# Shared feed-forward moved out of a pipelined loop, its last batch split into half banks and token tiles, and loop and experts joined in one program

## The chip, the cores and the metric

The kernel runs on one core of one Trainium2 chip. The metric is the device time of one execution in microseconds. A core has five engines with queues of their own: TensorE (PE, matmuls; PEld is its weight loads), VectorE (DVE), ScalarE (ACT), GpSimd (POOL) and SyncE (SP, which only issues transfers here). They meet through semaphores. ScalarE, GpSimd and SyncE issue DMAs, which 16 DMA engines carry out.

## The reference

Input x is 8 batches of 256 tokens of 512 features, the context has the same shape. Four layers follow each other, each added to x with a gate tanh(g):

```python
x = x + tanh(g_xattn[0]) * retention(layernorm(x), ctx)       # 4 heads
x = x + tanh(g_ffn[0]) * ffn_and_expert(layernorm(x))         # relu ffn + one expert matrix
x = x + tanh(g_xattn[1]) * attention(layernorm(x), ctx, ctx)  # over features, 8 heads
x = x + tanh(g_ffn[1]) * moe(layernorm(x))                    # below
```

The last layer has a shared part and 64 routed experts of capacity 256, of which each token uses six:

```python
su = x_flat @ w_shared_up; y_s, g_s = split(su, 2)
shared = silu(g_s) * y_s @ w_shared_down
scores = sigmoid(x_flat @ w_gate); topk_idx = top_k(scores, 6)
w = scores[topk_idx] / sum
pos = running number of the token in its expert; valid = pos < 256
out_r = silu(g_r) * v_r @ w_down      # per expert, on its gathered tokens
moe = shared + sum_k w_k * out_r[expert_k, pos_k]
```

The matrices of the shared part are 512 x 256 and 128 x 512; an expert's are 512 x 128 and 64 x 512. All matmuls but those of row maxima and of positions are in float32.

## The kernel before, in words

`build` opens three blocks one after the other; at the end of each block all engines meet. `setup_and_scores` makes the first attention's matrix and stores normalized x and values to HBM. `main_loop` carries the batches through three streams of units: **F** (first attention and first feed-forward: out, turn, gate, x1, turn2, logits, up, expert, down, with layer norms stats/norm, stats2/norm2, stats3/norm3), **T** (second attention) and **R** (routing and the shared feed-forward). The order of the units is one hand-written list, `ORDER` (L409). "T.V4+2" in it means that in step s the unit T.V4 runs for batch s - 2. F has lag 0, T lags 1 and 2, R lags 2 and 3, so that steps 3 to 7 hold all units and steps 8 to 10 the rest. Each engine runs its part of each unit in this order (`steps`, L462) and waits for the others only through semaphores; there is no other planner.

PSUM has eight banks. `quad` is four of them: a unit T.S0 to T.S7 fills it with scores (L1138), VectorE takes maxima of all four at once (`maxima`, L888), T.P and T.M turn those to rows; T.Q0 to T.Q7 fill it with shifted scores (L1160, L1163), ScalarE takes the exponential of all four (`exps`, L721), T.V multiplies by the values (L1178) into `t_pV`. GpSimd sums the exponentials over four such units per group (`sum_up`, L624: four additions in each of sum0a to sum0c, sum1a to sum1c), T.Z adds over partitions (L1187), T.A0 and T.A1 (`attended`, L903) scale, and T.add0 and T.add1 on GpSimd add to x (L632). `quad` has one occupant at a time (`QUAD`, L459). Three `work` banks go round among the other units (`WORK`, L458); a unit waits until the third before it is released.

R takes the norm of a batch (r_stats, rsqrt on GpSimd L610, r_norm), turns it (L1196), makes gates (r_gates), and VectorE finds the six experts, the position of each token in them and two kinds of addresses: r_sigmoid, r_hot, r_pos (matmuls L1214, L1215), r_slots, r_places. GpSimd then scatters: R.x0 to R.x3 send the 12 rows of token tiles and places to `xs_d` by three each (L644), R.send0 to R.send3 send 12 token numbers to `ids_d` (L658). R.up (L1206, eight matmuls of 256 columns, each run in two passes), R.shared (VectorE, L932 to L938), R.down0 and R.down1 (L1221, L943) are the shared feed-forward; the store to `acc_d` on SP's queue follows (L589), and behind batch 6's the first expert weights (L578). The last batch's token numbers are sent in the third block (L1329).

`experts` takes 32 pairs of experts: SP loads 4 x 128 rows of `xs_d` into one of four buffers (L1290) and the weights (L123, L124), TensorE transposes (e_pT, L1435), multiplies up (e_pU, L1447) and down (e_pD, L1458), ScalarE and VectorE evacuate, GpSimd scatters the results by token number to `y_d` (L1340), which needs `ids_d` back in SBUF (L1311, SP's queue between the rows of pair 3 and pair 4). The **final sum** goes over 16 token tiles: SP loads six rows per token in two parts (L1306) into eight buffers, VectorE runs six scalar_tensor_tensor in a chain (L1415), ScalarE stores (L1374).

## Time and profile before

| | us |
|---|---|
| median of 3 runs | 1253.87 (1252.85 to 1258.54) |
| the profiled execution, its own time | 1244.85 |
| its span | 1243.1 |
| TensorE busy (matmuls) | 1003.2 (81%) |
| VectorE busy | 707.4 (57%) |
| GpSimd busy | 611.1 (49%) |
| ScalarE busy | 300.8 (24%) |
| mean granted clock of TensorE | 0.91 of 2.4 GHz |
| moved by DMA | 252 MB, mean 203 GB/s |

Steps of the loop begin with the matmuls of F.out0. In the profile a busy time is the time with an instruction of that kind under way; matmul ends are modelled. The clock is what was granted: 1.00 is 2.4 GHz, 0.50 is 1.2 GHz. Where a row says "[x <-engine tile]", the engine was idle for x before it, until that released it; "issue" is idle time with no wait shown.

### The profile page before, as it was taken

To read this page: it belongs to the slowest core of one execution; us is meant where nothing else is said; L and a number is where in the kernel's file an instruction comes from. 1 tells how busy PE (TensorE), PEld (TensorE's weight loads), DVE (VectorE), ACT (ScalarE), POOL (GpSimd) and SP (SyncE) were. 2 spreads that over 40 slices of the span, in tenths; PEclk is the share of its full clock that TensorE was granted. 3 is DMA by queue.
4 is the path that set the end of the run, shared out by engine and by line. 5 is a ranking of instruction groups with operands and counts; after the bars stand their busy time and mean duration, and the time that the engine had idled before them with its cause. 6 is when DMAs were issued, how large, how long until landed. Compare 5 with 4: busy or idle time off the path is not lost. (4 is left out here: it accounts for less than half of the span.)

```text
span 1243.1 us, 16070 instructions
## 1 busy us (share of the span) xinstructions
PE 1003.2 (81%) x5966; PEld 562.1 (45%) x5966; DVE 707.4 (57%) x1241; ACT 300.8 (24%) x390; POOL 611.1 (49%) x588
## 2 busy tenths in 40 slices
...
PEclk9978999999999999999999986765999999999655
DMA  4892049487380652712403015035789899994796
GB/s 183 304 356 85 1 163 385 180 294 282 136 305 12 233 196 102 273 67 102 136 2 127 27 51 187 0 131 200 251 304 330 291 344 296 328 297 172 281 419 283
DMA packets 103834, 252.24 MB, mean 203 GB/s; under 512 B 14016, under 2 KB 14400, under 8 KB 102993
## 3 DMA queue, kind: packets, MB, share of 16 engines
...
## 5 line engine op out<-in xcount | busy, mean ns | idle before, releaser
L1340 POOL DMA_INDIRECT y_d<-e_eo,e_ids x128 | 124.8, 975 | 158.5 <-DVE e_eo L1395 126.8
L624 POOL TENSOR_TENSOR t_psum<-t_psum,t_probs 128x512 f32<-128x512 f32 x128 | 162.8, 1302 | 50.8 <-ACT t_probs L721 47.8
L888 DVE TENSOR_REDUCE t_nmx<-quad 128x4 f32<-128x2048 f32 x64 | 146.5, 2289 | 62.6 <-PE quad L1138 62.4
L721 ACT ACTIVATE t_probs<-quad 128x2048 f32<-128x2048 f32 x64 | 120.2, 1877 | 174.6 <-PE quad L1163 174.4
L644 POOL DMA_INDIRECT xs_d<-r_norm,r_xaddr x96 | 95.5, 995 | 28.0 <-issue 27.7
L658 POOL DMA_INDIRECT ids_d<-r_tokk,r_addr x84 | 82.7, 984 | 42.5 <-DVEq L1003 20.9
L1160 PE MATMUL quad<-b_qry,b_key 32*128 32x512 f32 x512 | 78.8, 687 | 19.9 <-ACT t_probs L721 13.6
L1389 DVE TENSOR_TENSOR e_hT<-e_pU,e_gate 128x256 f32<-128x256 f32 x32 | 13.6, 425 | 140.5 <-ACT e_gate L1356 98.2
L1435 PE MATMUL e_pT<-ident,e_xg 128*128 128x128 f32 x512 | 72.4, 286 | 22.9 <-DMA e_xg<-xs_d 22.4
L624 POOL TENSOR_TENSOR t_psum<-t_probs 128x512 f32<-128x512 f32 x64 | 82.3, 1320 | 11.7 <-ACT t_probs L721 9.7
L1138 PE MATMUL quad<-b_key,b_qry 32*128 32x512 f32 x512 | 74.7, 654 | 16.4 <-DVE t_nmx L888 13.2
L605 POOL TENSOR_TENSOR f_rstd<-f_veps,mhalf 128x2 f32<-128x2 f32 x24 | 17.0, 707 | 144.3 <-DVE f_veps L789 144.3
L1435 PEld LDWEIGHTS e_pT<-ident,e_xg 128*128 128x128 f32 x512 | 56.7, 144 | 61.0 <-issue 26.8
L1178 PE MATMUL t_pV<-t_probs,b_cT 128*32 128x512 f32 x512 | 68.2, 620 | 0.0
L1384 DVE COPY e_xT<-e_pT 128x512 f32<-128x512 f32 x64 | 44.1, 689 | 41.0 <-PE e_pT L1435 39.6
L1057 PE MATMUL work<-f_normT,wupT 128*128 128x256 f32 x256 | 61.3, 395 | 0.0
L1057 PE MATMUL work<-b_xnT,wg 128*128 128x256 f32 x256 | 59.7, 387 | 1.6 <-DVE f_zT L808 1.6
L1395 DVE COPY e_eo<-e_pD 128x512 f32<-128x512 f32 x64 | 44.3, 692 | 28.5 <-PE e_pD L1458 25.8
L1049 PE MATMUL work<-wo,f_zT 128*128 128x512 f32 x128 | 58.6, 601 | 1.3 <-issue 1.3
L1049 PE MATMUL work<-wexp,f_normT 128*128 128x512 f32 x128 | 58.7, 601 | 0.5 <-issue 0.5
L1049 PE MATMUL work<-wdnT,f_hT 128*128 128x512 f32 x128 | 58.8, 604 | 0.0
L1057 PEld LDWEIGHTS work<-f_normT,wupT 128*128 128x128 f32 x256 | 48.9, 196 | 17.0 <-issue 10.6
...
## 6 DMA issues: line engine op xcount, KB each, us to landing
...
```

Source lines behind the costliest of these rows:

```text
L624: ins = g_.tensor_tensor(psum0[:, q, :], first[:, q, :], probs[s % NP][:, q, :], ALU.add)
L644: g_.indirect_dma_start(out=xs_d, out_offset=bass.IndirectOffsetOnAxis(ap=xaddr[b % 2][:, t, k:k + 1], axis=0), in_=normR[b % 2][:, t, :], ...
L658: g_.indirect_dma_start(out=ids_d, out_offset=bass.IndirectOffsetOnAxis(ap=addr[b % 2][:, t, k:k + 1], axis=0), in_=tokk[b % 2][:, t, k:k ...
L721: A(probs[s % NP][:, :, :], quad[:, :, :], ACT.Exp, scale=SCALE1).then_inc(W["exp_ok"], 1)
L888: V.tensor_reduce(nmx[g][:, m, :], quad[:, :, :], axis=AX.X, op=ALU.max, negate=True).then_inc(W["mx_ok"], 1)
L1049: ins = mm(dst, lhs[:, k, t * P:(t + 1) * P], w[:, k, :], start=(k == 0), stop=(k == KC - 1))
L1057: ins = mm(dst[:, j * S:(j + 1) * S], w[:, k, o * P:(o + 1) * P], rhs[:, k, :], start=(k == 0), stop=(k == KC - 1))
L1138: ins = mm(quad[:, q, :], qry[b % 2][r, g, m * P:(m + 1) * P], key[b % 2][r, g, :], start=True, stop=True)
L1160: mm(quad[:, q, :], key[b % 2][r, g, n * P:(n + 1) * P], qry[b % 2][r, g, :], start=True, stop=False)
L1178: ins = mm(pV[q * HD:(q + 1) * HD, :], cT[:, n, r:r + HD], probs[s % NP][:, q, :], start=(n == 0), stop=(n == KC - 1))
L1340: g_.indirect_dma_start(out=y_d, out_offset=bass.IndirectOffsetOnAxis(ap=ids[:, HC * p + n:HC * p + n + 1], axis=0), in_=eo[u][:, n, :], i ...
L1435: last = tr(pT[t][:, k * P:(k + 1) * P], xg[u][:, HT * e + t, k * P:(k + 1) * P], ident[:, :])
```

## The change

R.up, R.shared and R.down leave the loop. Batch b's transposed norm is stored to HBM (R.keep, SP's queue) and the store to `acc_d` now comes right behind T.add1 (R.acc), without the shared part. The list `ORDER` has a new order for steps 0 to 5; steps 6 and 7 and all that follows is one list `ENDING`, with batch numbers. In it batch 7's second attention has units L: each S and Q is split into two half units of two `quad` banks each, with occupants kept per half (`quad_holders`); the sums over exponentials are four matmuls in each L.V (into a `work` bank), so GpSimd has no sum units for this batch; and norm, turn, gates, sigmoid, hot, pos, slots, places and row scatters go by token tile (0 and 1). r_places releases the row scatters (`route_ok`) before the token numbers are made (`ids_ok`). L.up0 to L.up7 are the shared feed-forward's first matmuls for all batches, into `quad`; ScalarE's Silu and one VectorE operation make `shT`. The three `with nc.Block()` become two: loop and experts are one program per engine, without a meeting of all engines in between; each first use of a buffer there waits for its own semaphores. The experts use `quad` and `work` as their PSUM banks, and one SBUF arena for the buffers of both. In the final sum TensorE makes the shared part's second matmul and, with diagonal matrices of the weights made by ScalarE, the first three rows; VectorE chains the other three and adds TensorE's result. The diff, cut:

```diff
+            loop, kept = main_loop(nc, io, outer, mid, {**constants, **weights, **drams})
+            final = experts(nc, io, out, outer, mid, {**constants, **weights, **drams, **kept})
+            with nc.Block() as block:
+                @block.sync
+                def _(sp):
+                    loop["sync"](sp)
+                    final["sync"](sp)
...
 ORDER = [(u.split("+")[0], int(u.split("+")[1])) for u in """
+F.out0+0 T.S0+1 F.out1+0 T.V4+2 R.acc+2 F.stats+0 T.S1+1 R.keep+2 F.norm+0 T.V5+2 T.V6+2 T.V7+2 T.sum1c+2 T.S2+1 F.turnA+0 F.turnB+0
+T.add1+2 T.A1+2 T.Z1+2 T.S3+1 T.P0+1 F.gateA+0 T.S4+1 F.next+0 F.gateB+0 T.S5+1 R.send0+3 T.M0+1 R.stats+2 F.x1a+0 R.norm+2 T.S6+1 F.x1b+0
+R.turnA+2 R.send1+3 R.turnB+2 T.Q0+1 R.gates+2 F.stats2+0 R.x1+3 R.send2+3 R.x2+3 T.Q1+1 F.keys+0 T.V0+1 F.turn2A+0 R.x3+3 F.turn2B+0
+T.sum0a+1 F.norm2+0 R.send3+3 T.V1+1 T.S7+1 F.logits+0 T.sum0b+1 F.best+0 F.upA+0 F.upB+0 T.P1+1 R.sigmoid+2 R.hot+2 F.weight+0 T.M1+1
+T.Q2+1 F.expert0+0 R.slots+2 T.Q3+1 T.cT+0 F.expert1+0 R.pos+2 R.places+2 T.Q4+1 T.sum0c+1 F.down0+0 T.Q5+1 R.x0+2 F.down1+0 F.stats3+0
+T.Q6+1 F.norm3+0 T.sum1a+1 T.sum1b+1 T.V2+1 T.Z0+1 T.V3+1 T.add0+1 T.Q7+1 T.A0+1
+""".split()]
+STEPS = 6
+ENDING = [(u.split("/")[0], int(u.split("/")[1])) for u in """
...
+T.Q5/6 R.places/5 F.down1/7 T.V2/6 T.Q6/6 T.Z0/6 T.V3/6 T.Q7/6 F.stats3/7 F.norm3/7 T.V4/6 T.sum1a/6 T.V5/6 T.A0/6 L.S0a/7 L.S0b/7 T.V6/6
+T.sum1b/6 L.S1a/7 L.S1b/7 T.sum1c/6 L.S2a/7 L.S2b/7 R.x3/4 T.add0/6 L.S3a/7 L.S3b/7 T.Z1/6 L.P0/7 L.S4a/7 R.acc/5 R.acc/6 L.S4b/7 R.send0/5
+R.x0/5 T.V7/6 L.M0/7 L.S5a/7 L.S5b/7 L.Q0a/7 T.A1/6 L.Q0b/7 L.S6a/7 T.add1/6 L.S6b/7 R.stats/6 R.send1/5 L.Q1a/7 R.norm/6 L.Q1b/7 L.S7a/7
+R.x1/5 R.x2/5 L.S7b/7 R.send2/5 R.turnA/6 R.send3/5 R.turnB/6 L.Q2a/7 L.Q2b/7 R.gates/6 L.add0/7 L.M1/7 L.Q3a/7 L.P1/7 L.V0/7 R.sigmoid/6
+L.V1/7 R.x3/5 R.hot/6 L.A0/7 L.Q3b/7 R.slots/6 L.stats0/7 R.places/6 L.V2/7 L.Q4a/7 R.x0/6 L.V3/7 L.Q4b/7 L.norm0/7 R.x1/6 L.Q5a/7 L.A1/7
+R.pos/6 L.Q5b/7 L.add1/7 L.sigmoid0/7 L.stats1/7 L.hot0/7 L.V4/7 L.norm1/7 R.x2/6 L.Q6a/7 L.slots0/7 L.Q6b/7 R.keep/5 L.V5/7 R.x3/6 L.Q7a/7
+L.Q7b/7 L.places0/7 R.keep/6 L.V6/7 L.rows0/7 L.rows1/7 L.V7/7 R.send0/6 L.turn0/7 R.send1/6 R.send2/6 L.sigmoid1/7 L.gates0/7 L.pos0/7
+L.turn1/7 R.send3/6 L.gates1/7 L.up0/7 L.up1/7 L.hot1/7 L.pos1/7 L.up2/7 L.up3/7 L.up4/7 L.up5/7 L.up6/7 L.up7/7 L.slots1/7 L.places1/7
 """.split()]
...
+        def r_keep(b):
+            sp.wait_ge(W["x4T_ok"], 2 * b + 2)
+            sp.dma_start(nrT_d[b, :, :].rearrange("p (k s) -> p k s", k=KC), normRT[:, :, :]).then_inc(W["nr_kept"], 16)
...
+                A(probs[n % NP][:, 2 * h:2 * h + 2, :], quad[:, 2 * h:2 * h + 2, :], ACT.Exp, scale=SCALE1).then_inc(W["exp_ok"], 1)
...
+        act.preload_act_table(ACT.Silu)
+        for b in range(NB):
+            act.wait_ge(W["su_mm"], b + 1)
+            A(shT[:, b, :], quad[:, b % G, S:2 * S], ACT.Silu).then_inc(W["es_ok"], 1)
...
+                V.tensor_reduce(nmx[g][:, m, 2 * h:2 * h + 2], quad[:, 2 * h:2 * h + 2, :], axis=AX.X, op=ALU.max, negate=True).then_inc(W["mx_ok"], 1)
...
+                for q in range(G):
+                    r = (g * G + q) * HD
+                    mm(pV[q * HD:(q + 1) * HD, :], cT[:, n, r:r + HD], probs[s % NP][:, q, :], start=(n == 0), stop=(n == KC - 1))
+                for q in range(G):
+                    ins = mm(z[q * HD:(q + 1) * HD, :], ones32[:, :], probs[s % NP][:, q, :], start=(n == 0), stop=(n == KC - 1))
...
+        for u in range(2):
+            sp.wait_ge(W[f"xscat{u}"], 16 * T * TOPK * (NB // 2))
+        sp.wait_ge(W["pv_mm"], 8 * NB)
+        for p in range(XB):
+            load_rows(p)
+        for u in range(2):
+            sp.wait_ge(W[f"scat{u}"], 16 * T * TOPK * (NB // 2 - u))
+        sp.wait_ge(ids_sent, 16 * T * TOPK)
...
+            for k in range(HALF):
+                done = A(diag[i % 2][:, k, :], ident[:, :], ACT.Copy, scale=comb_all[:, i, k:k + 1])
+            done.then_inc(diag_ok, 1)
...
+            V.tensor_tensor(acc[:, i, :], acc[:, i, :], pD[i % HC][:, :], ALU.add).then_inc(part_ok, 1)
...
+            mm(pD[i % HC][:, :], shT[:, i // T, (i % T) * P:(i % T + 1) * P], wsd[:, :], start=True, stop=False)
+            pe.wait_ge(part_in[u], 16 * uses(j, XB + OB))
+            pe.wait_ge(diag_ok, i + 1)
+            for k in range(HALF):
+                last = mm(pD[i % HC][:, :], diag[i % 2][:, k, :], parts[u][:, k, :], start=False, stop=(k == HALF - 1))
+            last.then_inc(half_mm, 1)
```

## Rows read from the trace of the kernel before

**Rows 1.** The page's forty slices of the span: granted clock and DMA share, in tenths.
```profile
PEclk9978999999999999999999986765999999999655
DMA  4892049487380652712403015035789899994796
```

**Rows 2.** Busy us by stretch: PE, PEld, DVE, ACT, POOL; then clock, DMA share, GB/s.
```profile
384.70:467.70 83.00, 81.48 (x477) 42.43 (x473) 63.71 (x116) 23.39 (x26) 59.95 (x55) 1.00 0.46 165
...
632.80:714.50 81.70, 80.66 (x472) 42.44 (x472) 63.08 (x115) 22.67 (x26) 59.13 (x54) 1.00 0.18 59
714.50:860.50 146.00, 83.70 (x424) 35.79 (x416) 78.74 (x146) 25.36 (x26) 108.83 (x99) 0.68 0.27 101
860.50:1161.20 300.70, 254.69 (x1792) 147.77 (x1792) 100.01 (x160) 86.47 (x161) 136.51 (x140) 0.97 0.83 284
1161.20:1243.10 81.90, 0.00 (x0) 0.00 (x0) 70.83 (x96) 0.00 (x0) 0.00 (x0) 0.50 0.89 359
```

**Rows 3.** Timeline of PE in steps 4 and 5: start us, us, instructions.
```profile
393.00 3.72 PE L1057 MATMUL work<-r_normT,wsu 128*128 128x256 f32 x16
396.65 1.14 PE L1138 MATMUL quad<-b_key,b_qry 32*128 32x512 f32 x8
...
410.70 3.70 PE L1049 MATMUL work<-wo,f_zT 128*128 128x512 f32 x8
414.34 1.14 PE L1138 MATMUL quad<-b_key,b_qry 32*128 32x512 f32 x8
...
419.13 1.02 PE L1221 MATMUL work<-wsd,r_shT 128*128 128x512 f32 x2
...
463.54 1.06 PE L1178 MATMUL t_pV<-t_probs,b_cT 128*32 128x512 f32 x8
```

**Rows 4.** Timeline of POOL around the end of step 4.
```profile
466.30 0.72 POOL L605 TENSOR_TENSOR f_rstd<-f_veps,mhalf 128x2 f32<-128x2 f32 x1 [0.64 <-DVE f_veps L789]
467.07 5.33 POOL L624 TENSOR_TENSOR t_psum<-t_probs 128x512 f32<-128x512 f32 x4
...
475.39 10.09 POOL L624 TENSOR_TENSOR t_psum<-t_psum,t_probs 128x512 f32<-128x512 f32 x8
485.44 1.27 POOL L632 TENSOR_TENSOR r_acc<-f_xs,t_att 128x512 f32<-128x512 f32 x1
```

**Rows 5.** Timeline of POOL: last row scatter, first and last of batch 7's token numbers.
```profile
850.13 0.98 POOL L644 DMA_INDIRECT xs_d<-r_norm,r_xaddr  x1 [0.30 <-issue]
861.20 0.97 POOL L1329 DMA_INDIRECT ids_d<-r_tokk,r_addr  x1 [10.09 <-POOLq L472]
...
875.26 0.97 POOL L1329 DMA_INDIRECT ids_d<-r_tokk,r_addr  x1 [0.30 <-issue]
```

**Rows 6.** Groups of instructions from 713 to 866 us: busy, mean ns, idle before.
```profile
L721 ACT ACTIVATE t_probs<-quad 128x2048 f32<-128x2048 f32 x10 | 18.8, 1878 | 39.0 <-PE quad L1163 39.0
L888 DVE TENSOR_REDUCE t_nmx<-quad 128x4 f32<-128x2048 f32 x8 | 18.3, 2290 | 8.7 <-PE quad L1138 8.6
```

**Rows 7.** Busy time by stretch, ten us of the drain.
```profile
760.00:770.00 10.00, 5.14 (x24) 1.54 (x24) 9.55 (x24) 1.11 (x1) 7.65 (x8) 0.54 0.36 135
```

**Rows 8.** Timeline of PE: last R.up, first expert transposes.
```profile
829.87 6.65 PE L1057 MATMUL work<-r_normT,wsu 128*128 128x256 f32 x16
...
866.26 3.87 PE L1435 MATMUL e_pT<-ident,e_xg 128*128 128x128 f32 x16 [22.44 <-DMA e_xg<-xs_d]
```

**Rows 9.** What POOL's sequencer ran at the end of the loop's block: ns, start.
```profile
L472 POOLq DRAIN  x1: 7167/7167/7167, 853.1 to 853.1; - x1
```

**Rows 10.** Timeline of SP's queue at the start of the experts.
```profile
860.50 2.84 SPq L1290 DMA_DIRECT2D e_xg<-xs_d  x4
877.42 0.33 SPq L1311 DMA_DIRECT2D e_ids<-ids_d  x1
```

**Rows 11.** Waits of SP's queue, 890 to 1150 us: total, times, longest.
```profile
SPq L110 <- PE e_pD L1458: 143.0, 21, 8.0
```

**Rows 12.** Busy time by stretch in the final sum.
```profile
1200.00:1229.00 29.00, 0.00 (x0) 0.00 (x0) 27.39 (x38) 0.00 (x0) 0.00 (x0) 0.50 1.02 419
1229.00:1243.00 14.00, 0.00 (x0) 0.00 (x0) 11.10 (x15) 0.00 (x0) 0.00 (x0) 0.50 0.31 120
```

More of the change, by code:

```diff
@@ L409 @@
 ORDER = [(u.split("+")[0], int(u.split("+")[1])) for u in """
-F.out0+0 T.sum1a+2 T.Q7+2 F.stats+0 F.out1+0 T.V4+2 T.sum1b+2 T.S0+1 T.V5+2 F.norm+0 R.up+3 T.cT+1 T.S1+1 R.shared+3
-F.gateA+0 T.sum1c+2 F.turnA+0 T.S2+1 T.A1+2 T.add0+2 R.send1+3 T.V6+2 T.V7+2 T.Z1+2 F.turnB+0 F.gateB+0 T.S3+1 T.P0+1
-T.add1+2 R.x0+3 R.stats+2 F.x1a+0 T.S4+1 R.x1+3 T.M0+1 R.norm+2 F.x1b+0 R.down0+3 T.Q0+1 R.turnA+2 F.stats2+0 R.turnB+2
-R.down1+3 F.next+0 R.x2+3 T.Q1+1 T.sum0a+1 R.gates+2 F.turn2A+0 F.norm2+0 R.send2+3 R.send3+3 F.turn2B+0 T.S5+1 R.x3+3 T.V0+1
@@ L414 @@
-F.logits+0 T.V1+1 F.best+0 T.S6+1 F.upA+0 R.sigmoid+2 T.S7+1 T.P1+1 F.upB+0 R.hot+2 T.Q2+1 F.weight+0 T.M1+1 F.expert0+0
-F.keys+0 T.Q3+1 F.expert1+0 R.pos+2 R.slots+2 R.places+2 T.Q4+1 T.sum0b+1 T.sum0c+1 F.down0+0 T.Q5+1 F.down1+0 T.V2+1
-R.send0+2 T.Q6+1 F.stats3+0 F.norm3+0 T.A0+1 T.Z0+1 T.V3+1
+F.out0+0 T.S0+1 F.out1+0 T.V4+2 R.acc+2 F.stats+0 T.S1+1 R.keep+2 F.norm+0 T.V5+2 T.V6+2 T.V7+2 T.sum1c+2 T.S2+1 F.turnA+0 F.turnB+0
+T.add1+2 T.A1+2 T.Z1+2 T.S3+1 T.P0+1 F.gateA+0 T.S4+1 F.next+0 F.gateB+0 T.S5+1 R.send0+3 T.M0+1 R.stats+2 F.x1a+0 R.norm+2 T.S6+1 F.x1b+0
@@ new lines @@
+STEPS = 6
+ENDING = [(u.split("/")[0], int(u.split("/")[1])) for u in """
+F.out0/6 T.S0/5 F.out1/6 T.V4/4 R.acc/4 F.stats/6 T.S1/5 R.keep/4 F.norm/6 T.V5/4 T.V6/4 T.V7/4 T.sum1c/4 T.S2/5 F.turnA/6 F.turnB/6
+T.add1/4 T.A1/4 T.Z1/4 T.S3/5 T.P0/5 F.gateA/6 T.S4/5 F.next/6 F.gateB/6 T.S5/5 R.send0/3 T.M0/5 R.stats/4 F.x1a/6 R.norm/4 T.S6/5 F.x1b/6
+R.turnA/4 R.send1/3 R.turnB/4 T.Q0/5 R.gates/4 F.stats2/6 R.x1/3 R.send2/3 R.x2/3 T.Q1/5 F.keys/6 T.V0/5 F.turn2A/6 R.x3/3 F.turn2B/6
+T.sum0a/5 F.norm2/6 R.send3/3 T.V1/5 T.S7/5 F.logits/6 T.sum0b/5 F.best/6 F.upA/6 F.upB/6 T.P1/5 R.sigmoid/4 R.hot/4 F.weight/6 T.M1/5
@@ new lines @@
+T.Q2/5 F.expert0/6 R.slots/4 T.Q3/5 F.expert1/6 R.pos/4 R.places/4 T.Q4/5 T.sum0c/5 F.down0/6 T.Q5/5 F.down1/6 F.stats3/6 T.Q6/5 F.norm3/6
+T.sum1a/5 T.sum1b/5 T.V2/5 T.Z0/5 T.V3/5 T.add0/5 T.Q7/5 T.A0/5 F.out0/7 T.S0/6 F.keys/7 F.out1/7 F.stats/7 T.V4/5 T.S1/6 F.norm/7 T.V5/5
+T.V6/5 T.V7/5 T.sum1c/5 T.add1/5 T.S2/6 T.A1/5 F.turnA/7 R.send0/4 T.Z1/5 T.S3/6 F.gateA/7 T.P0/6 F.turnB/7 T.S4/6 F.gateB/7 T.S5/6 T.M0/6
+R.x0/4 R.stats/5 T.cT/6 R.norm/5 F.x1a/7 T.Q0/6 R.x1/4 F.x1b/7 F.stats2/7 R.turnA/5 R.turnB/5 F.norm2/7 T.cT/7 T.Q1/6 T.V0/6 R.gates/5
@@ L961, in r_hot, with stage @@
+        def r_hot(part):
+            def stage(b):
+                each, ts, n = tiles(b, part)
+                for t in each:
                     ins = V.tensor_tensor(onehot[:, t, :, :], iota_e[:, :].unsqueeze(1).broadcast_to([P, TOPK, E1]),
@@ L982, in r_slots @@
                 link("r", ins)
[L983 to L992 removed]
+                link("r", V.tensor_reduce(pos[:, ts, :], ohp[:, ts, :, :], axis=AX.X, op=ALU.add))
@@ L1247, in experts @@
-def experts(nc, io, out, outer, v):
+                dve.sem_inc(W["ids_ok"], 1)
+                for t in each:
+                    V.tensor_scalar(comb_all[:, b * T + t, :], b_[:, t - each[0], :], wsum[:, 1, t:t + 1], tg_f[:, 1:2], ALU.mult, ALU.mult)
+            return stage
+        stages = {"F.stats": f_stats, "F.norm": f_norm, "F.stats2": f_stats2, "F.norm2": f_norm2, "F.best": f_best, "F.weight": f_weight,
+                  "F.stats3": f_stats3, "F.norm3": f_norm3, "T.P0": parts(0), "T.P1": parts(1), "T.A0": attended(0), "T.A1": attended(1),
+                  "R.stats": r_stats, "R.norm": r_norm, "R.sigmoid": r_sigmoid(None), "R.hot": r_hot(None),
+                  "R.slots": r_slots(None), "R.places": r_places(None),
+                  "L.P0": parts(0), "L.P1": parts(1), "L.A0": attended(0), "L.A1": attended(1)}
@@ new lines, in vector @@
+        for t in range(T):
+            stages[f"F.gate{'AB'[t]}"] = f_gate(t)
+            stages[f"F.x1{'ab'[t]}"] = f_res1(t)
+            stages[f"F.expert{t}"] = f_expert(t)
+            stages[f"F.down{t}"] = f_down(t)
+            stages[f"L.stats{t}"] = last_stats(t)
+            stages[f"L.norm{t}"] = last_norm(t)
+            stages[f"L.sigmoid{t}"] = r_sigmoid(t)
+            stages[f"L.hot{t}"] = r_hot(t)
+            stages[f"L.slots{t}"] = r_slots(t)
+            stages[f"L.places{t}"] = r_places(t)
```

1863 lines of the change are left out of this document (1012 added, 851 removed), and 3 rows, old and new, of the table RELEASES.

## The prediction

> **What bounds the kernel now.** I read the slices of the span first, the clock and DMA: TensorE's clock is nine tenths or more from the fifth slice to the twenty-third, falls, comes back, and is near half in the last three; the DMA engines fill up in the last third [rows 1]. The table by stage then gives numbers [rows 2]. Three steps of the loop lie between 384.70 and 632.80, so one takes 82.7 us; of the first one's 83.0 TensorE is busy 81.5, VectorE 64, GpSimd 60. From 714.50 to 860.50 the last batches drain: TensorE busy 84 of 146 us at clock 0.68, GpSimd 109. The experts take 300.7 us, the final sum 81.9 with VectorE alone. Four stages, four limits: matmuls; a chain through several engines; matmuls again; and, below, DMA.
>
> Sums go against the profiled execution (1244.85 us, span 1243.1). The median of the runs is 9.0 above it; I carry that offset over. A change under 0.5% (6 us) can't be told from none.
>
> **The loop: the shared feed-forward leaves.** R.up costs TensorE 3.65 us a batch (393.00 to 396.65) and each of two R.down at most 1.02 [rows 3]: 5.6 us. If TensorE were the only limit, a step would take 82.7 - 5.6 = 77.1. But freed time brings nothing where TensorE then waits, so I laid the new order along GpSimd's queue. Prices there: rsqrt 0.7 us; a sum unit of four additions 5.3 while VectorE normalizes, else 5.0 (10.09 for eight); an attention add 1.3 [rows 4]; one indirect DMA to the next 1.28 (861.20 to 875.26, eleven intervals) [rows 5]. Between the rsqrt of F.stats2 and T.Z1 the queue now holds twelve scatters (15.4), then sum0a, three scatters, sum0b, sum0c, three scatters (22.7), then rsqrt F.stats3, sum1a, sum1b, add0, rsqrt F.stats, sum1c (18.0): 56.1 us without a gap. From T.Z1 to the end of F.x1b TensorE has two gate units of 3.65, two x1 units of 3.65, four score units of 1.07 and two small ones (1.2) [rows 3]: 20 us. From the last matmul of a residual to the end of the rsqrt behind it is 3.5 us (F.down1 ends where T.V2 starts, 463.54; the rsqrt ends at 466.30 + 0.72) [rows 3, 4]. The ring closes in 80 us: TensorE will idle some 3 us ahead of T.Z1 in every step, and 1 us more in small waits. I take 80.3. That saves 2.4 us in each of steps 3 to 6 and loses 1 in step 2, which had no R.up to lose: **-8.6**. Ends: no wait at all, -23; waits as long as the matmuls saved, +1.
>
> Here a rule speaks against my reading. The Trainium skill (Perfetto Trace Analysis, Identifying the Most-Contended Engine) holds that matmul busy time misjudges TensorE and the busy share of weight loads judges it better. That share is 42.4 of 83.0 us, 51% [rows 2]; by that rule TensorE has headroom and the term would be 0. The starts in the table follow each other without a gap (393.00, 396.65; 410.70, 414.34), so I keep mine.
>
> VectorE and ScalarE lose r_shared and an Exp; both have slack, I cost that at nothing. R.keep stores 0.5 MB a batch, and on SP's queue R.acc (after T.add1, about 20 us into the step) and R.keep (after R.turnB, 35 us) now stand ahead of F.next; its loads are needed 40 us later, so they stay hidden, and DMA has room [rows 1]. T.cT waits in SP's queue for T.V7 of the batch before; only the next R.acc is behind it.
>
> **The last batch.** Step 7 starts 8.6 us earlier. From 632.80 to the last row scatter (850.13 + 0.97) it is 218.3 us now [rows 2, 5]. New: the rsqrt of F.stats3 of batch 7 ends 79 us into step 7 (70.4 of matmuls up to F.down1, 3.5, and 5 of the waits above). Behind it GpSimd has three sums of batch 6 (15.2), 39 scatters of batches 4 to 6 (49.9), four adds (5.2), three rsqrt (2.2) and batch 7's 12 row scatters (15.4): 88 us if it never waits. Batch 7's own six sum units are gone; TensorE makes the sums with four more matmuls per T.V. The other chain is VectorE and TensorE. A maximum costs 2.29 us and an exponential 1.88 [rows 6], in halves some 1.2 and 1.0, one half filled while the other is emptied: sixteen score halves (19) beside 17 us of batch 6's attention and routing, then 24 us of matmuls at full clock to L.V7, then stats, norm, turn, gates, sigmoid, hot, places by tiles (some 25), with L.up0 and L.up1 ahead of L.pos1 (7.3): 92. So both meet near 91, and the clock decides. It was 0.54 in a stretch of the drain with TensorE busy 5.1 of 10 us [rows 7], and one R.up there took 6.65 us instead of 3.65 [rows 8]. I take 96: last row scatter 175 us into step 7, **-43**. Ends: 166 (75 + 91, no waits) and 195 (all of L.V0 to L.V7 and L.up0, L.up1 at half). L.up2 to L.up7, 22 us, run while rows scatter and land: nothing; at half clock they take 40 and reach 15 us past the first expert rows.
>
> **No block end.** GpSimd's DRAIN at the end of the block takes 7.17 us [rows 9], and the first expert transposes start at 866.26 [rows 8], 15.2 after the last scatter. New: landing 2, load 5.8 (860.50 to 866.26), or L.up7's end: 9. **-6**. Behind batch 7's rows GpSimd issues the 12 address scatters of batch 6 and the 12 of batch 7, 24 x 1.28 = 31 us, and SP holds expert rows 4 and on behind them; before, the token numbers were fetched 17 us after the first rows (877.42) [rows 10]. Pair 4's rows are needed at about 46 us and can land at 41; the scatters of results start late and share the DMA with them. **+2**, ends 0 and +20.
>
> **Experts.** Same instructions, and SP waited 143 us for matmuls to free the buffers [rows 11]: TensorE sets the pace, 0.
>
> **Final sum.** VectorE goes from six operations of 0.72 us (27.39 for 38) [rows 12] to four per tile, TensorE gets four matmuls (3.6 us at full clock, by x1's four [rows 3]), ScalarE three small copies. But the DMA engines run at share 1.02 and 419 GB/s up to 1229. Reading 25.2 MB and writing 4.2 at 419 takes 70 us, 1.5 more for the start: the last part lands near 1232.4 on the old scale, 3.5 of sums and 2.4 of store follow, 1238.3 for 1243.1: **-5**. Without that limit 16 x 1.5 = 24 us would go. The Trainium skill (DMA: Bandwidth & Descriptors, Specifications) gives about 358 GB/s as a core's limit to HBM, by which the stage could not be shorter than 82 us and the term would be 0. The 419 GB/s measured in this very stage disagree.
>
> **Sum**: -8.6 - 43 - 6 + 2 - 5 = -61: 1184 for a profiled execution, 1253.87 - 61 = **1193 us** for the median.
>
> **Rivals.**
> - **No waits in the new order** (steps of 77.1, last batch 166): -23 - 52 - 6 - 5 = -86, 1168. For: the order of before leaves TensorE idle 1.5 us a step. Against: the ring above. Chance 0.17.
> - **Half clock in the last batch** (195): +20, 1213. For: 0.68 over the drain. Against: the V units now hold twice the matmuls. 0.17.
> - **Late token numbers** starve the experts, +20: 1211. 0.06.
> - **Steps not bound by TensorE** (the rule on weight loads): they stay at 82.7, 1202. 0.03. **No faster DMA than now in the final sum** (the rule on HBM): 1198. 0.02.
> - **The change doesn't do what it says**: a half waits for the other as whole banks do, 16 units x 1.2: 1212. 0.02.
> - **Slower than before**: T.Z1 waits for sum1c so long that steps 2 to 7 eat the gain. It decides from 80.3 + 61 / 6 = 90.5 us a step; if each of the 24 scatters of a step held the queue half a us longer, steps would take 92.3 and the time be 1265. The intervals in [rows 5] have no such delay. 0.03.
>
> The forecast has 0.5, its own range 1180 to 1206. Range **1166 to 1216**, from the rival without waits to half clock. Faster by over 0.5% 0.96, within it 0.01, slower 0.03.
>
> **What would show it.** Steps 3 to 6 near 80 us with TensorE idle ahead of T.Z1's matmuls, put down to GpSimd's t_psum; step 7 to last row scatter 175 us with GpSimd busy nearly throughout; no DRAIN; the first e_pT 9 us after the last row scatter and e_ids over 30 after it; a final sum of 77 us at 419 GB/s with VectorE idle a third of it. Steps of 77 refute the ring; a final sum under 70 us refutes the DMA bound; a clock of 0.5 from L.V0 to L.V7 refutes my last batch.

## The result, and the profile after

The changed kernel takes 1299.63 us (median of 4 runs, 1295.71 to 1304.06) where the kernel before, beside it, takes 1255.84: a ratio of 1.035, 95% interval 1.033 to 1.038. It is slower; 1193 was forecast, and 1216 was the top of the range. The profiled execution spans 1297.8 us, against 1243.1 before.

Stage table of the changed kernel, columns as in [rows 2]. Its lines are step 4; step 7 up to the rsqrt of F.stats3; from there to the last row scatter; from there to the first gate (ScalarE's first operation on a pair of experts); the expert pairs; the final sum.

```profile
409.40:498.10 88.70, 79.13 (x457) 39.86 (x453) 63.32 (x110) 22.89 (x24) 60.30 (x55) 0.96 0.45 161
675.60:765.10 89.50, 78.84 (x440) 40.64 (x440) 64.34 (x108) 21.75 (x23) 54.53 (x50) 0.94 0.11 39
765.10:880.90 115.80, 98.18 (x507) 44.81 (x500) 67.75 (x161) 27.91 (x37) 73.61 (x70) 0.81 0.47 173
880.90:926.20 45.30, 16.91 (x84) 12.64 (x83) 2.74 (x5) 2.28 (x6) 23.34 (x24) 0.66 0.36 123
926.20:1220.50 294.30, 247.61 (x1746) 143.62 (x1745) 98.36 (x158) 84.79 (x164) 124.70 (x128) 0.99 0.80 272
1220.50:1297.80 77.30, 59.35 (x126) 23.56 (x126) 47.07 (x64) 13.87 (x42) 0.00 (x0) 0.94 0.94 380
```

A step has grown from 82.7 us to 88.7 though TensorE has less to do in it. Step 7 begins at 675.6 instead of 632.8: 42.8 us are lost by then, 13.5 of them in step 3 (96.3 us). From there to the last row scatter it is 205 us instead of 218, so the new ending gives 13 back. Then 45.3 us pass up to the first gate, where it was 27 (851.1 to 878.2). The gates of the 32 expert pairs spread over 284 us instead of 273 (in a second pair of profiles, a0 and b0 below, over 269.5 and 271.0, so this loss did not come back), and the final sum takes 77.3 instead of 81.9.

Two places stand out. The first is the middle of every step from the fourth on. TensorE's timeline there:

```profile
543.52 1.95 PE L1206 MATMUL work<-wg,f_normT 128*128 128x8 f32 x16
545.33 5.30 PE L1214 MATMUL work<-f_normT,wupT 128*128 128x256 f32 x22
551.35 0.38 PE L1214 MATMUL work<-f_normT,wupT 128*128 128x256 f32 x1 [0.73 <-issue]
...
554.91 1.02 PE L1214 MATMUL work<-f_normT,wupT 128*128 128x256 f32 x4 [0.24 <-issue]
558.96 0.40 PE L1352 MATMUL work<-ident,t_nmp 128*128 128x128 bf16 x4 [3.03 <-DVE t_nmp L1022]
```

VectorE's timeline for the same microseconds:

```profile
546.38 2.29 DVE L1000 TENSOR_REDUCE t_nmx<-quad 128x4 f32<-128x2048 f32 x1 [8.12 <-remote]
554.96 0.25 DVE L950 MAX8 f_m<-work 128x8 f32<-128x8 f32 x2 [6.28 <-remote]
555.24 2.51 DVE L952 TENSOR_TENSOR f_gap<-f_m 128x2 f32<-128x2 f32 x1
...
558.59 0.32 DVE L1022 CAST t_nmp<-t_nmr 128x16 bf16<-128x16 f32 x1
```

And GpSimd's:

```profile
537.42 1.30 POOL L715 DMA_INDIRECT xs_d<-r_norm,r_xaddr  x1 [0.20 <-issue]
...
551.81 0.97 POOL L715 DMA_INDIRECT xs_d<-r_norm,r_xaddr  x1 [0.30 <-issue]
552.79 1.29 POOL L703 TENSOR_TENSOR t_psum<-t_probs,t_probs 128x512 f32<-128x512 f32 x1
```

By TensorE's records F.logits ended at 545.5, and F.best on VectorE waited only for it; it began at 554.96, with "remote" as its releaser. The matmuls of F.up, 0.22 us apart by right, stall one by one. Both go on until some 2 us behind the row of twelve indirect DMAs that GpSimd issues from 537.4 to 552.8. F.best, T.P1 and T.M1 follow late, and TensorE then stands idle for 3.0 us before T.M1. I call this **held completions**: TensorE's records say done, and its semaphores come later. As matmuls stall too, with no wait shown, more than the semaphores may be late; no run separates the two.

The kernel before has it as well, once in each of steps 3 to 7, and a wait table of its trace showed it before the change was made. Its second unit of F.up ends on TensorE at 442.05, and ScalarE takes it up 4.0 us later, 2 us behind a row of nine indirect DMAs. The last line is ScalarE's idle time before that unit over all these steps (total, times, longest us):

```profile
438.33 3.72 PE L1057 MATMUL work<-f_normT,wupT 128*128 128x256 f32 x16
446.09 0.60 ACT L703 ACTIVATE f_hT<-work 128x512 f32<-128x512 f32 x1 [8.12 <-remote]
ACT f_hT L703 <- remote: 39.2, 5, 8.1
```

The second is the experts' start. TensorE's timeline, from the last up-projection on:

```profile
884.71 3.62 PE L1214 MATMUL quad<-r_normT,wsu 128*128 128x256 f32 x16
888.68 1.07 PE L1683 MATMUL work<-ident,e_xg 128*128 128x128 f32 x8 [0.35 <-issue]
916.91 1.97 PE L1683 MATMUL work<-ident,e_xg 128*128 128x128 f32 x8 [27.16 <-ACT e_xT L1587]
```

ScalarE's beside it:

```profile
882.08 0.39 ACT L883 ACTIVATE r_shT<-quad 128x256 f32<-128x256 f32 x1 [3.69 <-PE quad L1214]
892.10 0.39 ACT L883 ACTIVATE r_shT<-quad 128x256 f32<-128x256 f32 x1 [9.63 <-remote]
915.98 0.39 ACT L883 ACTIVATE r_shT<-quad 128x256 f32<-128x256 f32 x1 [23.50 <-remote]
```

L.up7 ends at 888.3 on TensorE, and ScalarE's Silu on it starts at 915.98. GpSimd issued 42 indirect DMAs from 852.7 on with one break of 5 us; the last, a token number, went at 910.59. Full DMA engines do not explain it: they are full in the stretch shown before (share 1.05 from 545 to 550 us), but from 900 to 911 us their share is 0.02, and nothing is released. The transposes themselves begin 7.8 us after the last row scatter: that forecast (9) was good, and worth nothing, as the first gate came at 926.2.

Step 3 has a loss of its own. GpSimd's waits around its start (total, times, longest us) have this one:

```profile
POOL xs_d L715 <- DMA xs_d<-zero: 9.3, 1, 9.3
```

and TensorE's in the step this one:

```profile
PE quad L1295 <- DVE b_qry L990: 8.5, 1, 8.5
```

The first R.x0 now runs two steps behind its batch instead of three. It waits for the zeroes of xs, and the rsqrt of F.stats that T.S0 needs stands behind it.

### The profile page after: what moved, and what is told of

The parts are those of the page before. It is cut to its first block, busy times and chain, and to the rows that moved or that the text cites. A ratio compares the mean times of both kernels' runs of the same rounds, so it can differ in the third digit from the quotient of the medians.

```text
span 1297.8 us, 16371 instructions
## 1 busy us (share of the span) xinstructions
PE 1081.6 (83%) x6109; PEld 594.2 (46%) x6110; DVE 677.9 (52%) x1197; ACT 316.2 (24%) x447; POOL 583.4 (45%) x565
## 4 chain that ended last, share of the span: by engine, by line
PE 37%; another core or an unknown queue 16%; DVE 11%; issue 10%; POOL 10%; DMA 6%; ACT 3%; SPq 0%; ACTq 0%; POOLq 0%; DVEq 0%
PE work L1206 11%; POOL t_psum L703 7%; DMA e_eo<-y_d 5%; PE quad L1706 5%; PE work L1214 4%; PE work L1683 3%; PE quad L1365 3%; PE work L1695 2%; DVE t_nmx L1000 2%; PE quad L1295 2%; PE quad L1309 1%; POOL ids_d L744 1%; PE quad L1322 1%; ACT e_eo L1597 1%
## 5 line engine op out<-in xcount | busy, mean ns | idle before, releaser
L703 POOL TENSOR_TENSOR t_psum<-t_psum,t_probs 128x512 f32<-128x512 f32 x112 | 143.5, 1311 | 43.4 <-ACT t_probs L804 42.0
L1000 DVE TENSOR_REDUCE t_nmx<-quad 128x4 f32<-128x2048 f32 x56 | 128.0, 2285 | 55.1 <-remote 28.7
L804 ACT ACTIVATE t_probs<-quad 128x2048 f32<-128x2048 f32 x56 | 105.2, 1879 | 145.1 <-PE quad L1368 118.5
L715 POOL DMA_INDIRECT xs_d<-r_norm,r_xaddr x96 | 96.2, 1002 | 50.0 <-issue 26.7
L1683 PE MATMUL work<-ident,e_xg 128*128 128x128 f32 x512 | 71.7, 284 | 27.7 <-ACT e_xT L1587 27.2
L744 POOL DMA_INDIRECT ids_d<-r_tokk,r_addr x84 | 84.1, 1001 | 23.6 <-issue 22.9
L1635 DVE TENSOR_TENSOR e_hT<-work,e_gate 128x256 f32<-128x256 f32 x32 | 13.6, 425 | 151.9 <-ACT e_gate L1591 135.8
L1683 PEld LDWEIGHTS work<-ident,e_xg 128*128 128x128 f32 x512 | 56.2, 143 | 64.2 <-ACT e_xT L1587 33.0
L703 POOL TENSOR_TENSOR t_psum<-t_probs,t_probs 128x512 f32<-128x512 f32 x56 | 71.3, 1308 | 8.5 <-ACT t_probs L804 8.4
L1641 DVE COPY e_eo<-quad 128x512 f32<-128x512 f32 x64 | 44.3, 692 | 32.9 <-PE quad L1706 29.8
L1383 PE MATMUL t_pV<-t_probs,b_cT 128*32 128x512 f32 x448 | 57.7, 609 | 0.2
L1214 PEld LDWEIGHTS work<-b_xnT,wg 128*128 128x128 f32 x256 | 47.4, 190 | 16.5 <-issue 10.6
```

Of the source, the lines that this page charges most:

```text
L703: ins = g_.tensor_tensor(psum0[:, q, :], first[:, q, :], probs[s % NP][:, q, :], ALU.add)
L715: g_.indirect_dma_start(out=xs_d, out_offset=bass.IndirectOffsetOnAxis(ap=xaddr[b % 2][:, t, k:k + 1], axis=0), in_=normR[b % 2][:, t, :], ...
L744: g_.indirect_dma_start(out=ids_d, out_offset=bass.IndirectOffsetOnAxis(ap=addr[b % 2][:, t, k:k + 1], axis=0), in_=tokk[b % 2][:, t, k:k ...
L804: A(probs[s % NP][:, :, :], quad[:, :, :], ACT.Exp, scale=SCALE1).then_inc(W["exp_ok"], 1)
L1000: V.tensor_reduce(nmx[g][:, m, :], quad[:, :, :], axis=AX.X, op=ALU.max, negate=True).then_inc(W["mx_ok"], 1)
L1214: ins = mm(dst[:, j * S:(j + 1) * S], w[:, k, o * P:(o + 1) * P], rhs[:, k, :], start=(k == 0), stop=(k == KC - 1))
```

## The experiments

**Two kinds of chip.** Beside the first four experiments the kernel before took 1198.9 us, 57 less than above; beside others it took 1243.5, and 1198.8, 1198.8 and 1199.1. I call those with 1243 to 1256 the first kind and those with 1199 the second. One chip of the second kind was met twice, 50 minutes apart, and was the same both times; whether a chip can change its kind is not known. Ratios below are always against the kernel before on the same chip. All experiments are variants of one of the two kernels.

**e1_spread** (second kind). Scatters moved apart in the loop, and the same in the ending's first step:

```
-R.turnA+2 R.send1+3 R.turnB+2 T.Q0+1 R.gates+2 F.stats2+0 R.x1+3 R.send2+3 R.x2+3 T.Q1+1 F.keys+0 T.V0+1 F.turn2A+0 R.x3+3 F.turn2B+0
-T.sum0a+1 F.norm2+0 R.send3+3 T.V1+1 T.S7+1 F.logits+0 T.sum0b+1 F.best+0 F.upA+0 F.upB+0 T.P1+1 R.sigmoid+2 R.hot+2 F.weight+0 T.M1+1
+R.turnA+2 R.send1+3 R.turnB+2 T.Q0+1 R.gates+2 F.stats2+0 R.x1+3 R.send2+3 T.Q1+1 F.keys+0 T.V0+1 F.turn2A+0 F.turn2B+0
+T.sum0a+1 F.norm2+0 R.x2+3 R.send3+3 T.V1+1 T.S7+1 F.logits+0 T.sum0b+1 R.x3+3 F.best+0 F.upA+0 F.upB+0 T.P1+1 R.sigmoid+2 R.hot+2 F.weight+0 T.M1+1
```

> The changed kernel with one thing moved: in the loop the row scatters of R.x2 go behind T.sum0a and those of R.x3 behind T.sum0b, so that GpSimd issues no more than six indirect DMAs in a row there (twelve in a row before, 540 to 552 us of the step that begins at 498). Theory H (TensorE's completions are held back while a long row of indirect DMAs is being issued and landed: the semaphore of F.logits is seen 9 us late, F.best, T.P1 and T.M1 follow it): the steps 4 to 6 fall from 88.7 us to 80 to 83 each and the gaps inside F.upA and F.upB go; with step 3 and step 6 some 24 to 32 us in all, about 1270 us. Rival V (T.M1 waits because T.P1 stands behind F.best, F.logits and F.upB in the order of VectorE and TensorE, whatever GpSimd does): steps stay at 88 to 89, time 1297 to 1302. Rival G (GpSimd is only busy too long): sum0a comes earlier, but its later sums come later; steps 87 to 89.

1193.38 us, ratio 0.996 (0.994 to 0.999). Steps 3 to 6: 89.2, 83.4, 82.2, 83.6. On this chip it can't judge theory H, since here no completion is held in the first place (see a11_after).

**e2_bunched** (second kind). In the kernel before, R.x2 moved:

```
-R.down1+3 F.next+0 R.x2+3 T.Q1+1 T.sum0a+1 R.gates+2 F.turn2A+0 F.norm2+0 R.send2+3 R.send3+3 F.turn2B+0 T.S5+1 R.x3+3 T.V0+1
+R.down1+3 F.next+0 T.Q1+1 T.sum0a+1 R.gates+2 F.turn2A+0 F.norm2+0 R.x2+3 R.send2+3 R.send3+3 F.turn2B+0 T.S5+1 R.x3+3 T.V0+1
```

> The kernel before with one thing moved: R.x2 (three row scatters) goes from ahead of T.sum0a to ahead of R.send2, so that twelve indirect DMAs stand in a row there instead of nine; the order of the other engines is as it was. Theory H: the steps 3 to 6 grow from 82.7 us by 3 to 8 each, TensorE's last completions of F.logits and F.up reach the others late, time 1268 to 1290. Rivals V and G: GpSimd does the same work, only T.sum0a starts 3.8 us earlier and its scatters later: time within 3 us of the kernel before, 1253 to 1259.

1203.76 us, ratio 1.003 (1.001 to 1.005): rivals V and G on this chip, steps of 81.4 us.

**e3_x0late** (second kind). The changed kernel, R.x0 back to its old distance:

```
-R.turnA+2 R.send1+3 R.turnB+2
+R.turnA+2 R.x0+3 R.send1+3 R.turnB+2
...
-T.Q5+1 R.x0+2 F.down1+0
+T.Q5+1 F.down1+0
```

> The changed kernel with one thing moved: R.x0 goes back from two steps behind its batch to three, ahead of R.send1. It tells what step 3 (96.3 us) costs over the steps 4 to 6 (88.7): there GpSimd waits 9.3 us for the zeroes of xs in the first R.x0, ahead of the rsqrt that T.S0 needs, and TensorE waits 8.5 us for it. Theory X (that wait is the whole of it): step 3 falls to 88 to 90 us, the time by 6 to 9, to 1291 to 1294; the other steps stay at 88 to 89. Rival (the zeroes are late for R.x0 in the next step too, or the first step with scatters is longer for another reason): time stays at 1297 to 1302. Since three more scatters then stand among those of the middle of the step, theory H allows the other steps to grow by up to 2 us each.

1198.24 us, ratio 1.000 (0.998 to 1.002). Step 3 falls from 89.2 (a11_after) to 84.1 and steps 4 to 6 are 85.5, 85.2, 85.1 instead of 84.2, 83.9, 85.2. The wait is gone, its gain is 5 us in step 3, of which two or three are given back in the others; in the total it can't be told from none.

**e4_drained** (second kind). After each three scatters of batches 6 and 7 GpSimd waits until they have landed:

```
+pool.wait_ge(W[f"xscat{b % 2}"], 16 * (T * TOPK * (b // 2) + (n + 1) * per))
...
+if k % 3 == 2:
+    pool.wait_ge(ids_sent, 16 * (TOPK * t + k + 1))
```

> The changed kernel with waits added to GpSimd alone: after each three indirect DMAs of the batches 6 and 7 (rows and token numbers) it waits until they have landed, so that there are never more than three under way from 800 us on. It adds about 2 us for each three, some 30 us of GpSimd's time at the end. Theory H: TensorE's completions are passed on at once: the shared up-projections end 10 us earlier on ScalarE, and the first expert pair's gate comes within 12 us after the first expert transposes (37.6 us in the changed kernel), while the last token number is scattered some 20 to 30 us later than at 911; time between 1285 and 1310, as the added waits eat what is won. Rival A (ScalarE and VectorE are late at the experts' start because of the store of batch 7 or a table load): the distance from first expert transposes to first gate stays above 25 us. Rival L (the row loads of 4 MB hold TensorE): it stays above 20 us too, since the loads are the same.

1229.42 us, ratio 1.026 (1.023 to 1.029). First transposes 862.5, first gate 871.1: 8.5 us, but 7.2 without the waits on such a chip, so this says nothing on H. What it does price is the queue: the last token number goes out at 903.3 instead of 876.8 (a11_after), and the total is 29 us up.

**a0_after, b0_before, e5_both, e6_oldorder** (side by side, first kind). e5 joins e1's and e3's moves. e6 takes the order that the loop had before, for seven steps, without R.up, R.shared, R.down0 and R.down1, with R.acc+2 behind R.x0+3 and R.keep+2 behind R.turnB+2; the ending then begins with batch 7:

```
-STEPS = 6
+STEPS = 7
...
-F.out0/7 T.S0/6 F.keys/7
+F.out0/7 T.sum1a/5 T.Q7/5 T.sum1b/5 T.S0/6 F.keys/7
...
-T.V6/5 T.V7/5 T.sum1c/5 T.add1/5 T.S2/6 T.A1/5 F.turnA/7 R.send0/4 T.Z1/5
+T.V6/5 T.V7/5 T.sum1c/5 T.add0/5 T.add1/5 T.S2/6 T.A1/5 F.turnA/7 T.Z1/5
```

> The changed kernel itself, beside the others. The first four experiments had the kernel before at 1198.9 us, 55 less than the 1253.9 of the first profile, so what is read from one chip need not hold on this one. Theory H in its narrowed form (the late completions come with the chip, not with the order alone): if the kernel before takes about 1199 here, the changed one takes 1198 to 1206, its steps 4 to 6 about 85 us, its first expert pair's gate comes 7 to 8 us after the first expert transposes, and all pairs take about 8.0 us; if the kernel before takes about 1254, the changed one takes 1296 to 1304 with steps of 88.7. Rival (the loss is the order's alone): 3.5% over the kernel before on either chip, 1240 where that takes 1199.

> The kernel before itself, with a profile of this chip, to have its stages beside those of the changed kernel. Theory H narrowed: where it takes about 1199 us in all, the loop is within 5 us of the first profile (step 7 begins at 628 to 634), and what is gone is the waiting of ScalarE for pU at the experts: nearly every pair takes 7.8 to 8.0 us instead of 8.8 on average (a gain of 30), and the final sum about the same. Rival (everything is some 4% faster): each stage shrinks by 4%, the pairs to 8.4.

> The changed kernel with both earlier moves: R.x0 three steps behind (ahead of R.send1), R.x2 behind T.sum0a, R.x3 behind T.sum0b. Where completions are prompt (kernel before at 1199): steps 3 to 6 at 82 to 84 us, 1186 to 1192. Where they are held (before at 1254): steps 3 to 6 at 80 to 84 instead of 96.3 and 88.7, some 35 us less than the changed kernel, 1258 to 1268, with the experts' part as slow as in the changed kernel.

> The changed kernel with the order of the loop as it was before, for the first seven steps, less the three feed-forward stages; the last batch, the experts and the final sum are as changed. It tells the price of the new order from that of the feed-forward: before, a step held 3.6 + 3.7 + 3.7 + 1.3 us of the feed-forward on TensorE, VectorE and ScalarE and took 82.7. Theory O (the feed-forward was on TensorE's path and the new order gives it back): steps 3 to 6 at 75 to 79 us, step 7 begins 15 to 25 us earlier than in the kernel before, and the whole is 3 to 4% faster than the kernel before. Rival P (GpSimd's work or VectorE's sets the step, with or without the feed-forward): steps at 81 to 83, step 7 begins within 5 us of the kernel before, the whole is 1 to 2% faster than it.

The kernel before: 1243.45 us. a0 1285.45, ratio 1.035 (1.031 to 1.039): the result again. b0 1.000. e5 1281.95, ratio 1.031 (1.027 to 1.034): steps 3 to 6 take 90.1, 91.8, 92.0 and 86.2 where a0's take 97.3, 90.0, 88.7 and 90.4. Step 3 is better without its wait for the zeroes, the rest is not. e6 **1235.23, ratio 0.993 (0.990 to 0.995)**: steps 3 to 6 at 82.0, 82.0, 81.9, 79.9, step 7 begins at 628.2 where b0 has 634.8 and a0 680.6. The order of the loop alone thus costs 52 us on this chip. The old order is not free of holds either: in each of e6's steps 3 to 6 the second unit of F.up reaches ScalarE late, here in step 5, by 4.2 us:

```profile
517.15 3.72 PE L1210 MATMUL work<-f_normT,wupT 128*128 128x256 f32 x16
525.02 0.60 ACT L782 ACTIVATE f_hT<-work 128x512 f32<-128x512 f32 x1 [8.24 <-remote]
```

The same order has steps of 78.5 us on the second kind (e12_best below), where ScalarE starts on this unit at once, so holds go with some 3.5 us of a step of 82.0.

Why e5 failed, on TensorE's timeline in its step 4:

```profile
450.71 1.09 PE L1200 MATMUL work<-ident,f_norm 128*128 128x128 f32 x8
455.39 1.94 PE L1383 MATMUL t_pV<-t_probs,b_cT 128*32 128x512 f32 x8 [3.58 <-issue]
```

and on ScalarE's:

```profile
451.18 0.28 ACT L834 ACTIVATE r_eg<-work 128x128 f32<-128x128 f32 x1 [2.81 <-remote]
453.46 1.88 ACT L804 ACTIVATE t_probs<-quad 128x2048 f32<-128x2048 f32 x1 [2.00 <-remote]
457.70 0.60 ACT L776 ACTIVATE f_normT<-work 128x512 f32<-128x512 f32 x1 [2.37 <-remote]
```

R.x0, R.send1, R.x1 and R.send2 now stand together with one rsqrt of 0.7 us among them, twelve scatters again, and the hold moved under R.gates, T.Q1 and F.turn2. My edit broke up one run and made another.

**e7_best, e8_noids, e9_drained, e10_bunched** (second kind). e9 and e10 are e4 and e2 again. e7 is e6 with one more move:

```
-L.rows0/7 L.rows1/7 L.V7/7 R.send0/6
+L.rows0/7 R.send0/6 L.rows1/7 L.V7/7
```

e8 is the changed kernel without 24 scatters, and without the waits of SP for them. It leaves out the token numbers of batches 6 and 7, so the expert results of these two batches go nowhere and its output is not the reference's:

```
+if b == LB - 1:
+    return
...
-for t in range(T):
-    for k in range(TOPK):
-        g_.indirect_dma_start(out=ids_d, out_offset=bass.IndirectOffsetOnAxis(ap=addr[last % 2][:, t, k:k + 1], axis=0),
```

> The old order in the loop as in e6_oldorder, and R.send0/6 (three token-number scatters) ahead of L.rows1, where GpSimd waits some 5 us for L.places1. All theories: the last token number goes out 3.8 us earlier, and with it the token numbers' load, the first row of y and, where completions are held until GpSimd's scatters are through, the first gate. 0.990 to 0.996 of the kernel before where completions are held (0.993 in e6_oldorder), 0.97 to 0.98 where they are prompt, since the loop has 20 us less than in the changed kernel there.

> The changed kernel without the token-number scatters of the batches 6 and 7 (24 indirect DMAs of 128 numbers each, the last that GpSimd issues before the experts), so that its output lacks the right places for these two batches' rows. Theory H on a chip with held completions: from the first expert transposes to the first gate 7 to 14 us instead of 37, first row of y 25 to 35 us earlier, time 1250 to 1262 where the changed kernel takes 1285 to 1300. Rival A and L (the store of batch 7, the row loads of 4 MB or a table load hold TensorE): that distance stays above 25 us, the time falls by less than 10. On a chip with prompt completions both expect a distance of 7 to 8 us and a time some 10 to 17 us less than the changed kernel's, since the token numbers come 30 us after the rows there.

> The same kernel as e4_drained, which met a chip with prompt completions (first expert transposes to first gate 8.6 us with it). If this chip holds completions: theory H expects 8 to 14 us here too, with the scatters going on for 30 us more than in the changed kernel beside it, so that not their number but their standing close together holds TensorE; time within 15 us of the changed kernel. Rival N (any indirect DMA under way holds them until the last of them): the first gate comes only after the last token number, 40 us or more after the first transposes, time 30 us or more above the changed kernel's.

> The same kernel as e2_bunched, the kernel before with twelve indirect DMAs in a row in each step. On the chip with prompt completions it was 0.3% slower. If this chip holds completions: theory H expects the steps 3 to 6 at 84 to 90 us instead of 82.7, and 1% to 2% over the kernel before; rivals V and G: within 0.4%.

e7 takes 1155.68 us, **ratio 0.963 (0.958 to 0.967)**: it beats both kernels. Steps 3 to 6 take 78.5 each. e8: 1192.79, 0.994 (0.991 to 0.996). e9: 1228.18, 1.025 (1.022 to 1.028). e10: 1202.89, 1.002 (1.000 to 1.004). The chip was again of the second kind, so e9 and e10 confirm e4 and e2 and no more (from first transposes to first gate it is 10.0 us in e9, and 10.1 in e14 below).

**a11_after, e12_best, e13_noids, e14_drained**, and then **e15_noids, e16_best**: the same kernels again, to have the changed kernel on a chip of the second kind, or the others on one of the first.

> The changed kernel itself. If the kernel before takes about 1199 us (completions prompt): 1198 to 1206, steps 4 to 6 at 82 to 85.5 us, step 3 some 8 longer for the zeroes, first expert transposes to first gate 7 to 8 us. If the kernel before takes 1243 to 1254 (held): 1.030 to 1.040 of it, as twice already.

> The kernel of e7_best again. If completions are prompt: 0.960 to 0.966 of the kernel before, as measured. If held: 0.987 to 0.995, since the run of 24 token numbers still holds TensorE for some 20 us at the experts' start.

> The kernel of e8_noids again (no token-number scatters for the batches 6 and 7). If held: theory H expects 7 to 14 us from the first expert transposes to the first gate where the changed kernel has 36 to 38, and a time 25 to 40 us under the changed kernel's beside it; rivals A and L: over 25 us, and less than 10 under it. If prompt: 7 to 8 us and some 7 to 12 us under the changed kernel.

> The kernel of e9_drained again (never more than three indirect DMAs under way from the batch-6 scatters on). If held: theory H expects 8 to 14 us from the first expert transposes to the first gate, with a time within 15 us of the changed kernel's; rival N (any indirect DMA under way holds) over 40 us, and a time 30 us or more above. If prompt: 8 to 9 us and 1228, as measured.

> The kernel of e8_noids a third time, in the hope of a chip with held completions (kernel before at 1243 to 1254 us). There: theory H expects 7 to 14 us from the first expert transposes to the first gate where the changed kernel has 36 to 38, and 0.995 to 1.015 of the kernel before; rivals A and L: over 25 us, and 1.02 or more. Where they are prompt: 7 to 8 us and 0.990 to 0.995.

> The kernel of e7_best a third time. Held: 0.985 to 0.995 of the kernel before, the first gate some 30 us after the first expert transposes. Prompt: 0.960 to 0.967.

All were of the second kind. **a11: 1200.55 us, ratio 0.999 (0.997 to 1.002): on such a chip the change makes no difference.** e12 0.963 (0.960 to 0.967), e16 0.960 (0.956 to 0.965); e13 0.992, e15 0.993; e14 1.026. The experts' start in a11, TensorE's timeline:

```profile
853.45 3.62 PE L1214 MATMUL quad<-r_normT,wsu 128*128 128x256 f32 x16
856.90 1.04 PE L1683 MATMUL work<-ident,e_xg 128*128 128x128 f32 x8
858.27 1.21 PE L1683 MATMUL work<-ident,e_xg 128*128 128x128 f32 x8 [0.33 <-ACT e_xT L1587]
```

and ScalarE's:

```profile
857.10 0.39 ACT L883 ACTIVATE r_shT<-quad 128x256 f32<-128x256 f32 x1 [3.07 <-PE quad L1214]
```

The Silu follows its matmuls at once, with the same 24 token numbers being issued beside it (the last at 876.8). The kernel is the same, its scatters are issued at the same rate, and only on one kind of chip are the completions held.

The stages on the second kind, from the profiles (us; e10 stands for the kernel before, 0.2% off it):

| | e10 | a11 (changed) | e12 (old loop order) |
|---|---|---|---|
| step 7 begins | 627.9 | 654.7 | 618.4 |
| from there to the start of the last row scatter | 213.5 | 191.5 | 188.3 |
| to the first gate | 26.7 | 17.9 | 16.7 |
| first to last gate | 240.9 | 248.6 | 244.9 |
| to the end | 92.0 | 87.5 | 87.9 |

## Why the prediction was wrong

**The loop (-8.6 forecast).** This step failed: the loop got 42.8 us longer. With the order unchanged, the removal of the feed-forward starts step 7 earlier by 6.6 us (e6 against b0) and 9.5 (e12 against e10). That this is near 8.6 is luck, for 2.4 us a step was what a ring in the new order would leave over. In the old order it is 0.7 us a step on the first kind (82.7 to 82.0) and 2.9 on the second (81.4 to 78.5), where TensorE's busy time falls by 5.3 us and 2.4 of new waits for VectorE's maxima and ScalarE's exponentials take back half. What I took for a free choice, the new order, is what costs: 52 us on the first kind, 36 on the second (a11 against e12). The 36 are 9 in steps 0 to 2, 11 in step 3 and 18 in steps 4 to 6, less 1 at the start. I laid it along GpSimd's queue only, as a ring of 80.3 us. The ring's own wait is there: T.Z1 waits 2.1 us a step for t_psum, where I had 3. But other terms were missing.

Waits on VectorE, for one. TensorE's largest waits in steps 4 to 6 of a11 (total, times, longest us):

```profile
PE work L1392 <- POOL t_psum L703: 6.4, 3, 2.1
PE quad L1295 <- DVE t_nmx L1000: 4.8, 6, 1.0
PE work L1206 <- DVE f_xs L967: 4.3, 3, 1.4
```

and of e12 (steps 3 to 5):

```profile
PE quad L1291 <- DVE t_nmx L996: 4.3, 3, 1.4
PE quad L1361 <- ACT t_probs L800: 3.1, 3, 1.0
```

With the smaller ones the new order waits 18 us in three steps, the old one 7. The steps are 84.4 and 78.5 long; TensorE's busy time, 77.9 against 76.1, and a clock of 0.98 against 1.00 are most of the rest. I looked at what VectorE loses, costed that "at nothing", and never laid the new order along its queue.

The zeroes of xs, 8.5 us in step 3. The prediction counted R.x0's scatters in the queue, and not the wait in front of them that the earlier step makes real. Its worth is near 5 us at most (e3).

Held completions: the steps 4 to 6 of a0 exceed those of a11 by 5 to 6 us, and e6's steps 3 to 5 exceed e12's by 3.5, so they make the new order 52 us dearer instead of 36. The 1.5 us a step that the prediction had TensorE idle in the order of before belong to them too: in e10 it is 0.2. I said of the rival "slower than before" that it decides from 90.5 us a step and that the intervals between scatters show no delay. The place was wrong: the scatters were punctual, and the delay fell on TensorE's semaphores.

The first steps. I left 0, 1 and 2 as they were but for 1 us; they take 9.7 more together (59.9, 81.1, 80.7 for 58.0, 75.5, 78.5). Why is not worked out.

**The last batch (-43 forecast).** Measured from the start of step 7: -13 in the result, -16 on the first kind again (a0, b0), -22 to -25 on the second. The mechanism was right, its size was not: 175 us were forecast, 205 (the result), 199 (a0), 192 (a11) and 189 (e12) measured, to the end of that scatter. In a11 the rsqrt of F.stats3 ends 88 us into step 7, not 79: up to the end of F.down1 TensorE is busy for 75.8 us instead of 70.4, at a clock of 0.94, and waits 9 instead of 5, the longest time 3.7 ahead of R.pos. It is 88 in e12 too, so this is the ending's own order and not the loop's. From there it is 104 us, not 96: GpSimd waits 8.1 us once for VectorE's t_att in L.add0. On the first kind that wait is 12.3, and completions held under a run of fifteen scatters (798.7 to 818 in the changed kernel's profile) lie ahead of it; how much of it they make up is not shown. The clock from there to the last row scatter was 0.81 in the result and 0.80 in a11, so half clock did not decide.

**No block end (-6).** On the second kind the first transposes start 9.8 us after the last row scatter (a11) where it was 15.2 (e10), and up to the first gate it is -9 to -10: right and small. On the first kind +17 to +18 up to the first gate instead, under held completions. **Late token numbers (+2, ends 0 and +20).** Leaving the 24 scatters out brings 0.8% or 9.6 us (a11 against e13) and 248.6 us between first and last gate become 241: the term was 8 to 10, within its ends. **Experts (0).** +8 on the second kind, wholly those token numbers: without them (e13) it is 241 us, as in e10. On the first kind +11 in the result and -1.5 in a0 against b0. **Final sum (-5).** 77.3 us for 81.9, so -4.6; VectorE busy 47 of it. DMA is at share 0.94 and 380 GB/s over the whole stage. Step right, and with it my choice of the measured 419 GB/s. The Trainium skill (DMA: Bandwidth & Descriptors, Specifications) has about 358 GB/s as the limit, by which the stage would last 82 us; the trace disagrees, with 77.3.

**Of the chances**: 0.96 for faster rested on step 7 alone and on steps that could only win. The rule on weight loads had 0.03; its forecast for steps (82.7) was nearer than mine, and for the wrong reason, as taking the matmuls away in the old order does shorten a step on the second kind, from 81.4 to 78.5 us.

**What stays open.** That held completions come from GpSimd's indirect DMAs is inferred: they start some six DMAs into a run, end 2 to 4 us behind its last, move with the run (e5), and are shorter behind nine DMAs (4 us, in the kernel before and e6) than behind twelve (9 us, in the result). On a chip of the first kind neither leaving scatters out nor draining them was measured, for no such chip came again. Why only some chips show it is not known; nor whether e7 beats the kernel before there (e6, which has all but one of its edits, does, by 0.7%).
